# Output stage of a graph layer: row sums from the aggregation's add, variance by a Square pass on ScalarE, and the normalisation one tile later

## What is computed

```python
x = x + _gat(_layernorm(x), edges, ...)        # aggregation of layer 2 ends here
h = _layernorm(x) @ W0.T + b0                  # W0: 96 x 768
h = 0.5 * h * (1 + tanh(c * (h + 0.044715 * h**3)))
x = x + h @ W1.T + b1                          # W1: 768 x 96
```

## Time and profile before

| | us |
|---|---|
| median of 3 runs | 4394.83 (4390.88 to 4399.89) |
| the profiled execution, its own time | 4393.57 |
| its span, first to last instruction | 4391.8 |
| PE, DVE, ACT, POOL busy over the span | 3519.7, 2160.0, 1302.9, 1088.3 |
| first and last add of the aggregation (L1627) | 3850.01, 4372.06 |

### The profile page before, as it was taken

The page is one execution under the profiler, slowest core; times in us unless marked ns, Lnnn a source line. Parts: engine busy times, 40 slices in busy tenths (PEclk is TensorE's granted clock), DMA queues, the critical chain, the costliest instruction groups (busy, mean ns, idle before and its releaser), DMA issues. The chain is left out here.

```text
span 4391.8 us, 67315 instructions
## 1 busy us (share of the span) xinstructions
PE 3519.7 (80%) x21804; PEld 2144.6 (49%) x21805; DVE 2160.0 (49%) x5207; ACT 1302.9 (30%) x2233; POOL 1088.3 (25%) x1396
## 2 busy tenths in 40 slices
PE   4850018999999999999999999999999900078988
PEld 3640005665556655565556655665556500055665
DVE  8877135334433444344433444344434200289998
ACT  3531104223332333223322333233322200034444
POOL 2447731000000000000000000000000067466665
PEclk9975559999999999999999999999999955589999
DMA  8862001111111111111111111111111000178887
GB/s 257 256 194 60 3 16 49 52 38 49 41 45 52 40 42 42 56 37 46 38 52 37 52 40 43 53 38 43 43 55 39 24 6 1 28 208 230 235 230 207
DMA packets 147719, 338.13 MB, mean 77 GB/s; under 512 B 81378, under 2 KB 82178, under 8 KB 140030
## 3 DMA queue, kind: packets, MB, share of 16 engines
q1 hardware_dynamic: 112047, 240.87, 18.1%
q0 software_dynamic: 34240, 93.39, 8.9%
q10 hardware_dynamic: 1175, 0.05, 0.0%
HBM read 266.08 MB, written 124.25 MB: 89 GB/s over the span
## 5 line engine op out<-in xcount | busy, mean ns | idle before, releaser
L934 POOL DMA_INDIRECT lay_rows<-parts,lay_idx x200 | 210.1, 1051 | 2533.1 <-PE lay_pz L1177 1615.8
L1211 PE MATMUL lay_pm<-lay_zh,w1h 128*128 128x500 f16 x1920 | 717.6, 374 | 26.5 <-DVE lay_h L1097 21.2
L1212 PE MATMUL lay_pm<-lay_zl,w1h 128*128 128x500 f16 x1920 | 717.9, 374 | 2.1 <-issue 1.7
L1213 PE MATMUL lay_pm<-lay_zh,w1l 128*128 128x500 f16 x1920 | 717.8, 374 | 0.0
L1018 DVE SCALAR_TENSOR_TENSOR lay_zl<-lay_pz,lay_zh 128x400 f16<-128x400 f32 x600 | 319.6, 574 | 708.5 <-ACT lay_zh L1128 708.5
L1128 ACT ACTIVATE lay_zh<-lay_pz 128x400 f16<-128x400 f32 x600 | 298.3, 504 | 1054.7 <-PE lay_pz L1177 1050.9
L1137 ACT ACTIVATE lay_ex<-lay_pm,b1c,scale 128x500 f32<-128x500 f32 x320 | 245.6, 768 | 869.5 <-PE lay_pm L1213 869.5
L1235 PE MATMUL lay_pm<-w2h,lay_gh 128*128 128x512 f16 x1280 | 484.9, 379 | 0.0
L1235 PE MATMUL lay_pm<-w2h,lay_gl 128*128 128x512 f16 x1280 | 483.9, 378 | 0.0
L1235 PE MATMUL lay_pm<-w2l,lay_gh 128*128 128x512 f16 x1280 | 483.4, 378 | 0.0
L1053 DVE TENSOR_SCALAR lay_ex<-lay_ex,scale 128x500 f32<-128x500 f32 x320 | 153.7, 480 | 568.2 <-ACT lay_ex L1137 568.2
(11 more groups left out here) (275 smaller groups left out, 5860.0 us busy)
## 6 DMA issues: line engine op xcount, KB each, us to landing
x<-in_x_dram SPq DMA_DIRECT2D x20, 1500.0 KB, 6.7
out_x<-x SPq DMA_DIRECT2D x100, 288.0 KB
out_own<-h SPq DMA_DIRECT2D x100, 288.0 KB
out_dram<-out_x SPq DMA_DIRECT2D x100, 288.0 KB
nrm_xb<-in_x_dram SPq DMA_DIRECT2D x20, 1344.0 KB
parts<-nrm_parts SPq DMA_DIRECT2D x20, 1344.0 KB
h<-lay_h SPq DMA_DIRECT2D x80, 336.0 KB
nrm_w<-in_L_gnn_W_dram SPq DMA_DIRECT2D x6, 1024.0 KB, 19.3
```

Source lines behind the costliest of these rows:

```text
L1211: pe.matmul(o, c.w1h[:, d, cols], zh[:, d, h], start=(d == 0), stop=False)
L1212: pe.matmul(o, c.w1h[:, d, cols], zl[:, d, h], start=False, stop=False)
L1213: ins = pe.matmul(o, c.w1l[:, d, cols], zh[:, d, h], start=False, stop=(d == DC - 1))
```

## The change

DVE no longer runs `bn_stats` and `bn_aggr`. Its add of the aggregation becomes a `scalar_tensor_tensor` that also writes out the row sums, from which two small instructions make minus the mean, and minus the mean over the square root of D. ACT makes the variance with a Square activation over the tile, with scale D^-0.5 and that bias, and its row sums (`spread2`). POOL adds 1e-5 itself, an eighth instruction in its chain, which now waits for ACT (`dev_ready`). On ACT `xn` moves from the end of iteration n to the start of iteration n+1, and the Square of tile n takes its place at the end. All that follows `xn` (transposes, copy, hidden layer, gelu, output, last add, store) lies one tile further behind: the store of tile n-5 in iteration n, where it was n-4.

```diff
         att = m.sb("att", [OE, AB, OT])
-        stats, mv = m.sb("stats", [OT, 2, 2, 6]), m.sb("mv", [OT, 2, 2])
+        dev, total, spread2 = m.sb("dev", [OT, D]), m.sb("total", [OT, 2]), m.sb("spread2", [OT, 2])
+        nms, eps = m.sb("nms", [OT, 2]), m.sb("eps", [OT, 1])
         ve, nm, rough, sq, rstd, shift = (m.sb(n, [OT, 2]) for n in ("ve", "nm", "rough", "sq", "rstd", "shift"))
 ...
         power, spare = m.sb("power", [OT, 1]), m.sb("spare", [1, 1])
 ...
         TILES = NO
-        FIRST, LAST = -AHEAD, TILES + 3
+        FIRST, LAST = -AHEAD, TILES + 4
 ...
                     load_slots(of, range(GT * part // LOADS, GT * (part + 1) // LOADS))
-                t, at, there, ok = tile_at(grp, j, -4)
+                t, at, there, ok = tile_at(grp, j, -5)
                 if ok:
 ...
                     for lo, hi in row_parts(OT):
 ...
             nc.gpsimd.memset(onehalf[:], 1.5).then_inc(posed, 1)
+            nc.gpsimd.memset(eps[:], EPS).then_inc(posed, 1)
             nc.gpsimd.memset(rows[:], 0.0).then_inc(posed, 1)
-            pool.wait_ge(posed, 4)
+            pool.wait_ge(posed, 5)
 ...
                 t, at, there, ok = tile_at(grp, j, AHEAD)
 ...
                     rough_, sq_, ve_, rstd_ = (a[:, at % 2:at % 2 + 1] for a in (rough, sq, ve, rstd))
-                    nw = Chain(pool, newton, 6 * t)
-                    pool.wait_ge(ve_ready, t + 1)
+                    nw = Chain(pool, newton, 7 * t)
+                    pool.wait_ge(dev_ready, t + 1)
+                    nw.link(nc.gpsimd.tensor_tensor(ve_, spread2[:, at % 2:at % 2 + 1], eps[:], ALU.add))
                     nw.link(nc.gpsimd.tensor_tensor(rough_, ve_, power[:], ALU.pow))
 ...
                     nw.link(nc.gpsimd.tensor_tensor(sq_, sq_, ve_, ALU.mult))
 ...
                 col = slice(b, b + 1)
-                lc = Chain(dve, chain, 3 * t)
+                lc = Chain(dve, chain, t)
                 if ok:
 ...
                     dve.wait_ge(own_added, t + 1)
-                    nc.vector.tensor_tensor(x[:, at], x[:, at], pa[0:OT, 0:D], ALU.add).then_inc(x2_ready, 1)
-                    dve.wait_ge(x2_ready, t + 1)
-                    for half in range(2):
-                        lc.put(nc.vector.bn_stats(stats[:, b, half], x[:, at, half * (D // 2):(half + 1) * (D // 2)]))
-                    lc.wait()
-                    nc.vector.memset(spare[:], 0.0)
-                    lc.link(nc.vector.bn_aggr(mv[:, b], stats[:, b].rearrange("p a b -> p (a b)")))
                     if beyond(t, 2):
                         dve.wait_ge(norm_ready, t - 1)
-                    nc.vector.tensor_scalar(nm[:, col], mv[:, b, 0:1], -1.0, None, ALU.mult)
-                    nc.vector.tensor_scalar(ve[:, col], mv[:, b, 1:2], EPS, None, ALU.add).then_inc(ve_ready, 1)
-                    assert lc.n == 3, lc.n
+                    nc.vector.scalar_tensor_tensor(out=x[:, at], in0=x[:, at], scalar=1.0, in1=pa[0:OT, 0:D], op0=ALU.mult,
+                                                   op1=ALU.add, accum_out=total[:, col]).then_inc(x2_ready, 1)
+                    dve.wait_ge(x2_ready, t + 1)
+                    nc.vector.tensor_scalar(nms[:, col], total[:, col], -1.0 / D ** 1.5, None, ALU.mult)
+                    nc.vector.tensor_scalar(nm[:, col], total[:, col], -1.0 / D, None, ALU.mult).then_inc(mean_ready, 1)
                 if next_group(grp):
 ...
                         slot_math(grp + 1)
 ...
                     rows_now(grp + 1, 1)
-                tg, ag, _, okg = tile_at(grp, j, -3)
+                tg, ag, _, okg = tile_at(grp, j, -4)
                 gb = ag % 2
 ...
                                                    op1=ALU.mult).then_inc(t_ready, 1)
-                tf, af, _, okf = tile_at(grp, j, -4)
+                tf, af, _, okf = tile_at(grp, j, -5)
                 if okf:
 ...
                     nc.vector.tensor_tensor(x[:, af], x[:, af], po[0:OT, 0:D], ALU.add).then_inc(o_ready, 1)
 ...
             def iteration(grp, j):
-                tg, ag, _, okg = tile_at(grp, j, -3)
+                t, at, _, ok = tile_at(grp, j, -1)
+                if ok:
+                    act.wait_ge(norm_ready, t + 1)
+                    if beyond(t, 2):
+                        act.wait_ge(turned, t - 1)
+                    b = at % 2
+                    nc.scalar.activation(xn[:, b], x[:, at], ACT.Identity, bias=shift[:, b:b + 1], scale=rstd[:, b:b + 1])\
+                        .then_inc(xn_ready, 1)
+                tg, ag, _, okg = tile_at(grp, j, -4)
                 if okg:
 ...
                     nc.scalar.activation(th[:, ag % 2], u2[:, ag % 2], ACT.Tanh, scale=GELU_C).then_inc(th_ready, 1)
-                t, at, _, ok = tile_at(grp, j, -1)
+                t, at, _, ok = tile_at(grp, j, -2)
                 if ok:
 ...
                     if beyond(t, 2):
 ...
                         .then_inc(xt_ready, 1)
-                th_, ah_, _, okh = tile_at(grp, j, -2)
+                th_, ah_, _, okh = tile_at(grp, j, -3)
                 if okh:
 ...
                     if beyond(th_, 2):
 ...
                 if ok:
-                    act.wait_ge(norm_ready, t + 1)
+                    act.wait_ge(mean_ready, t + 1)
+                    if beyond(t, 1):
+                        act.wait_ge(dev_ready, t)
                     if beyond(t, 2):
-                        act.wait_ge(turned, t - 1)
+                        act.wait_ge(norm_ready, t - 1)
                     b = at % 2
-                    nc.scalar.activation(xn[:, b], x[:, at], ACT.Identity, bias=shift[:, b:b + 1], scale=rstd[:, b:b + 1])\
-                        .then_inc(xn_ready, 1)
+                    nc.scalar.activation(dev[:], x[:, at], ACT.Square, bias=nms[:, b:b + 1], scale=D ** -0.5,
+                                         accum_out=spread2[:, b:b + 1]).then_inc(dev_ready, 1)
 ...
                         .then_inc(agg_done, 1)
-                t, at, _, ok = tile_at(grp, j, -1)
+                t, at, _, ok = tile_at(grp, j, -2)
                 if ok:
 ...
                     if beyond(t, 1):
 ...
                     ins.then_inc(turned, 1)
-                t, at, _, ok = tile_at(grp, j, -2)
+                t, at, _, ok = tile_at(grp, j, -3)
                 if ok:
 ...
                     if beyond(t, 1):
 ...
                     ins.then_inc(h_done, 1)
-                t, at, _, ok = tile_at(grp, j, -3)
+                t, at, _, ok = tile_at(grp, j, -4)
                 if ok:
```

More of the change, by code:

```diff
@@ L1398, in stage_output @@
         sems = ("par_in", "turned_w", "w_ready", "init", "posed", "slots_in", "idx_ready", "mask_ready",
-                "looked", "weights_ready", "att_ready", "agg_done", "x2_ready", "ve_ready", "norm_ready", "newton", "xn_ready",
+                "looked", "weights_ready", "att_ready", "agg_done", "x2_ready", "mean_ready", "dev_ready", "norm_ready", "newton", "xn_ready",
                 "turned", "xt_ready", "h_done", "u_ready", "t_ready", "th_ready", "g_ready", "o_done", "o_ready",
@@ L1402, in stage_output @@
         (par_in, turned_w, w_ready, init, posed, slots_in, idx_ready, mask_ready, looked, weights_ready,
-         att_ready, agg_done, x2_ready, ve_ready, norm_ready, newton, xn_ready, turned, xt_ready, h_done, u_ready, t_ready,
+         att_ready, agg_done, x2_ready, mean_ready, dev_ready, norm_ready, newton, xn_ready, turned, xt_ready, h_done, u_ready, t_ready,
          th_ready, g_ready, o_done, o_ready, own_added, chain, setup, gelu, prep, bias_in, held, paused) = (
@@ L1572, in _ @@
             ch.wait()
-            nc.vector.memset(stats[:], 0.0).then_inc(w_ready, 1)
+            nc.vector.memset(total[:], 0.0).then_inc(w_ready, 1)
             def slot_math(grp):
```

## The result

| | before | after |
|---|---|---|
| median of 4 runs, us | 4392.87 (4390.88 to 4399.89) | 4604.51 (4590.11 to 4610.37) |
| ratio, 95% interval | | 1.0474 (1.0447 to 1.0501) |
| profiled execution: time, span, us | 4393.57, 4391.8 | 4590.11, 4588.4 |

What follows compares the result with a forecast made beforehand. DVE bound the stage at 5.30 us a tile; afterwards the longest closed wait loop, loop 2 at 7.45, would. 98 tiles x (7.45 - 5.30) = 211 us plus 4 for the deeper pipeline gave 4610 us, range 4500 to 4700.

Steps and rivals of the forecast that it cites:

- loop 2: Gather, PE to hidden layer, ACT's reads and Square, POOL's chain, next gather; once per two tiles: 14.91 us, 7.45 a tile.
- loop 3: SP's x load waits for the store just issued, once per tile: landing 4.5 plus 2.7, 7.2 us.
- loop 1: ACT's Square, POOL's chain, `xn` and ACT's other work wait for each other once per tile: 6.67 us.
- four turns in ten: Share of loop 2 turns in which PE's piece runs at the lower clock, 2.78 us more each.
- The chain on POOL: POOL's eight instructions per tile with gaps: 3.04 us, bounds 2.7 and 3.6; 0.35 less if L1525 escapes DVE's L1649.
- the rival that the stores bind: SP's stores set the pace, from a landing of 4.75 us; at 5.5, 8.2 us a tile, 4683 us; chance 0.14.
- PE at the lower clock in every tile: Rival: waits for gathers throttle PE each time, 16.58 us per two tiles, 8.29 a tile, 4692 us; chance 0.12.
- Loop 1 alone: Rival: gathers land early enough and PE keeps its clock; 4533 us, or 4500 with the short chain; chance 0.25.
- The gain: DVE without `bn_stats` needs some 1.15 us less, about 3.9 us a tile, useful only if nothing else exceeds 5.30.
- faster: Rival: DVE's 1.15 us comes back until PE's 4.7 us bind, needing loop 1 below 5.30; 4336 us; chance 0.02.
- The deeper pipeline: The pipeline is one tile deeper at its end, adding 4 us.
- The signs: Profile after: 14 adds in 106 us, DVE near 53%, PE waiting for most gathers, clock near 0.8.

Runs made afterwards that it cites:

- e4: Kernel before, with SP storing each tile one iteration later (tile n-5 instead of n-4): 4548.92 us, ratio 1.0325.
- e5: Changed kernel with ACT's order altered, Square of tile n first and `xn` of tile n-1 last: 4544.83 us, ratio 1.0332.
- e1: Changed kernel with the x load one tile later (tile n+3 instead of n+4): 4591.51 us, ratio 1.0439.
- e10: Changed kernel with the last add writing to five tiles of its own, so the x load needs no landed store: 4588.67 us, ratio 1.0449.
- e11: e10 plus, on PE, the aggregation of tile n+1 moved between hidden layer and output: 4513.9 us, ratio 1.0270.
- e9: Changed kernel with the ACT order of e5 and the last add's own buffers of e10: 4430.3 us, ratio 1.0074 against the kernel before.
- e2: Changed kernel with `xn` moved to the end of ACT's iteration, behind the Square of the next tile: 4592.46 us, ratio 1.0448.
- e7: Changed kernel with the x load one tile later and the aggregation of tile n+1 last in PE's iteration: 4638.66 us, ratio 1.0556.
- e12: Kernel before, with the last add writing to buffers of its own, nothing else: 4393.99 us, ratio 0.9995.

## Why the prediction was right

- **The mechanism.** Three closed loops, the longest deciding, and no sum of them: each was measured alone, loop 2 at 7.15 us, loop 3 at 6.85, loop 1 at 6.43, and all three together at 7.19. The forecast had 7.45, 7.2 and 6.67, in the same order.
- **Loop 2's terms.** PE's piece from the aggregation to the end of the hidden layer ran 88 times between 3900 and 4540 us: 51 times at the full clock, 3.05 us in the mean, and 37 times partly or wholly at the lower one, 4.93 us. The two pieces of the turn above (columns as in the earlier trace rows), and one that waited and kept its clock:

```profile
4194.83:4199.56 4.73, 4.73 (x23) 3.51 (x24) 3.10 (x8) 1.88 (x3) 1.82 (x5) 0.64 0.81 247
4200.69:4203.70 3.01, 3.00 (x23) 2.18 (x22) 0.95 (x1) 0.45 (x3) 1.89 (x8) 1.00 0.63 173
```
```profile
4237.46 1.07 PE L1753 MATMUL out_pa<-out_rows,out_att 128*100 128x512 f32 x2 [2.87 <-DMA out_rows<-h,out_idx_now]
```

  The 37 turns that begin with the gather of a slow piece sum, in their means, to gap 0.75, gather to PE's start 4.98, piece 4.93, reads 0.51, Square 1.02, handover 0.09, chain 2.49: 14.77 us, where I had 14.91. The sum is right, two of its terms are not, and that they cancel is luck. I took four turns in ten at 2.78 us more; it was 37 in 44, more than eight in ten, at 1.88 more, since the clock rose again within most of the pieces: 1.58 us a turn and not 1.11. And the chain was 0.55 us shorter in these turns than the 3.04 taken. Where no piece was slow, from 4230 to 4271 and from 4491 to 4516 us, one aggregation followed the other by 6.8 and 6.3 us in the mean, against 7.27 over the whole stretch and 6.43 for loop 1 alone. So much of what sets loop 2 above loop 1 is the clock; this is read from the trace, no run separates it.
- **The chain on POOL.** L1525, 541 ns in the mean, is now L1528 and takes 230. This agrees with the rule of the Trainium skill ("SBUF — State Buffer", section "SBUF: two separate sides") that I set against the mean: away from its neighbour on DVE it is short. In the kernel before 61 of 85 (3900 to 4350 us) began while L1649 ran, in the changed kernel 8 of 88 (3900 to 4540 us) while L1647 did. But the stretch did not vanish. It went to the instruction that now starts beside DVE's L1647, the first of the chain, 408 ns in the mean against the 0.20 taken: 36 of 88 began while L1647 ran, whose inputs all lie in SBUF, and took 0.68 us in the mean; 30 began while the last add L1663 ran, which reads PSUM, and each took 0.18. So the chain lies between the two values, 2.76.
- **Loop 3.** I placed it "just under loop 2". e4 and e5 have it at 6.85 where I had 7.2. W was 3.7 and 4.8 us in e5's two rounds, with 4.5 taken. At 6.85 the rival that the stores bind (0.14) falls, and e1 and e10, 4592 and 4589, exclude it.
- **PE at the lower clock in every tile** (0.12). Its name says every tile, its sum, 13.80 + 2.78 for two tiles, one slow piece in each turn. Every tile is excluded by the 51 of 88 pieces at the full clock. One slow piece a turn is nearly what came, 37 in 44; but it cost 1.88 us and not 2.78 (six of the 37 took over 5.7 us), and a tile 7.19 us and not 8.29. The mechanism was there to a larger part than my 0.12 allows. As argued, a slow piece leaves little idle time behind it: after 36 of the 37 the next one ran at the full clock. The Trainium skill's passage on oscillation ("TensorE: Matmul & The Clock Gate", section "HAM oscillation — how this bites in real kernels") fits the clock falling behind waits for gathers, but in nearly every turn here and not in every tile.
- **Loop 1 alone** (0.25), 4533 or 4500 us: not in the changed kernel. e11, where it is alone, gives 4514, between the two.
- **The gain.** DVE's busy time went from 100.57 us over 20 adds to 369.13 us over some 94 tiles (3880 to 4560 us), 3.9 us a tile as forecast. It is of no worth here, and e9 shows it is of none even with the three loops open; what takes their place, POOL's own work or the gather's way through PE and ACT, is not shown. I had not priced that: the rival "faster" named only loop 1 as its condition.
- **Sizes at the ends.** The deeper pipeline cost 8 us at the end, about one tile at the new pace, where I wrote 4. The pace cost 190 us, where I wrote 211. So in the profiled execution the change cost 197 us against 215; the median, 4604.51, comes nearer to 4610 because the other three executions took 13 to 20 us longer than the profiled one, and so far it is luck.
- **The signs.** The adds came 14 or 15 times in 106 us; DVE 53%; PE waited for the gather in 62 of 88 tiles; clock 0.87 where I said near 0.8; SP's issue of the store did wait for DVE, 16 times, so it was not the stores.

## What to carry to other kernels

Before an operation is moved to an idle engine, write down every closed chain of "stands behind" and "waits for" that the new order makes, with the number of tiles that one turn covers; the pace is the longest turn divided by its tiles, and busy shares do not show it. Loops do not add, so opening one of several tied ones gains next to nothing, as e1, e2 and e10 show (12 to 16 of 212 us), and an edit that opens one may close another (e7). A transfer that waits for a landing should not be the next thing its queue does after issuing it: one iteration's difference cost the kernel before 150 us in e4 (4548.92 against 4399.05 on that chip), and buffers of their own for the stored tiles take the wait away (e5 to e9, 1.0332 to 1.0074) and cost nothing by themselves (e12).

## What the runs showed of the hardware

- Writing out the accumulator is an instruction of its own, 194 ns on ACT and 82 ns on DVE, behind the operation itself (927 and 952 ns). On ACT it begins some 0.1 us before the recorded end of the Square, so that the two together take 1.02 us.
- A 100x1 operation on POOL takes 0.18 to 0.19 us alone and 0.93 in e11's turn above, where it starts just behind DVE's product of two SBUF inputs; beside a DVE add that reads PSUM it stays at 0.18. Which instruction of a chain is stretched changes with the phase of the two engines, so its mean belongs to the schedule and not to the instruction.
- 35 us of waiting in SP's queue cost nothing in the kernel before, and 56 us were lost when its loads were issued a tile later.
- How long PE waited does not tell by itself at which clock it goes on: behind 2.87 us without work (4237.46 us) the piece ran at the full clock, behind 1.16 us, and 1.50 us three operations earlier (4034.12 us), it took 4.72 us at a mean of 0.64.
